# Expert outputs scaled at the PSUM evacuation and scattered with addition into two accumulators

## What is computed

```
xn = layernorm(x)
s  = attention branch of RWKV form: k, v, r projections of token-shifted xn,
     a running exponential average over the 512 tokens (the scan), then (r * rwkv) @ Wo.T
probs = softmax(xn @ w_router.T)              # 16 experts
top_w, top_e = top_k(probs, 4); top_w /= sum(abs(top_w))
moe = 0
for e in range(16):
    coeff = sum(where(top_e == e, top_w, 0))
    h = silu(xn @ w_gate[e]) * (xn @ w_up[e])
    moe = moe + coeff[:, None] * (h @ w_down[e])
out = x + s * silu(moe)
```

## Time and profile before

| | |
|---|---|
| median of 3 runs | 364.33 us (363.87 to 364.96) |
| profiled execution, first to last instruction | 374.3 us |
| PE, DVE, ACT, POOL busy | 83%, 76%, 39%, 61% of the span |
| granted TensorE clock, mean | 0.946 of full speed |
| moved by DMA | 48.81 MB, mean 130 GB/s |

### The profile page before, as it was taken

The page is one execution under the profiler, slowest core; times in us unless marked ns, Lnnn a source line. Parts: engine busy times, 40 slices in busy tenths (PEclk is TensorE's granted clock), DMA queues, the critical chain, the costliest instruction groups (busy, mean ns, idle before and its releaser), DMA issues.

```text
span 374.3 us, 4815 instructions
## 1 busy us (share of the span) xinstructions
PE 310.6 (83%) x1162; PEld 183.0 (49%) x1163; DVE 282.9 (76%) x534; ACT 146.0 (39%) x222; POOL 227.3 (61%) x231
## 2 busy tenths in 40 slices
...
GB/s 248 300 343 348 345 5 0 90 164 44 154 42 83 84 48 94 143 78 70 73 78 135 42 84 80 79 93 132 73 79 85 213 189 331 48 234 125 133 112 113
DMA packets 37894, 48.81 MB, mean 130 GB/s; under 512 B 3756, under 2 KB 33453, under 8 KB 37872
## 3 DMA queue, kind: packets, MB, share of 16 engines
...
...
## 4 chain that ended last, share of the span: by engine, by line
PE 43%; DVE 33%; issue 8%; DMA 4%; POOL 3%; ACT 3%; another core or an unknown queue 2%; SPq 1%; DVEq 1%; POOLq 0%; ACTq 0%
PE ps L588 36%; DVE wbig L1042 6%; DVE ohA L924 5%; PE ps L690 3%; PE ps L677 3%; DVE ohB L922 2%; POOL y_rows L411 2%; DMA xg<-xn_rows,tok_idx 2%; DMA woT<-woT_in 2%; DVE arena L954 1%; POOL xg L404 1%; PE ps L597 1%; DVE arena L815 1%; DVE arena L949 1%
## 5 line engine op out<-in xcount | busy, mean ns | idle before, releaser
L588 PE MATMUL ps<-wbig,arena 128*128 x576 | 206.3, 499 | 10.6 <-DVE arena L949 6.8
L588 PEld LDWEIGHTS ps<-wbig,arena 128*128 128x128 f32 x576 | 105.2, 195 | 74.5 <-issue 67.4
L411 POOL DMA_INDIRECT y_rows<-arena,s_idx x56 | 62.2, 1110 | 42.3 <-ACT arena L541 25.5
L404 POOL DMA_INDIRECT xg<-xn_rows,g_idx x64 | 70.3, 1099 | 22.8 <-issue 17.0
L954 DVE TENSOR_TENSOR arena<-arena,ps 128x512 f32<-128x512 f32 x36 | 24.5, 682 | 41.9 <-ACT arena L536 25.9
L536 ACT ACTIVATE arena<-ps 128x512 f32<-128x512 f32 x36 | 21.5, 597 | 87.0 <-PE ps L588 53.2
L588 PE MATMUL ps<-arena 128*128 128x512 f32 x96 | 47.1, 638 | 1.0 <-DVE arena L815 1.0
L949 DVE COPY arena<-ps 128x512 f32<-128x512 f32 x36 | 24.8, 690 | 26.3 <-PE ps L690 18.2
L541 ACT COPY arena<-ps 128x512 f32<-128x512 f32 x36 | 21.1, 585 | 45.8 <-PE ps L588 35.9
L690 PEld LDWEIGHTS ps<-ident,arena 128*128 128x128 f32 x144 | 18.4, 145 | 22.6 <-issue 19.3
L588 PEld LDWEIGHTS ps<-arena 128*128 128x128 f32 x96 | 18.6, 202 | 21.5 <-issue 19.4
(11 more groups left out here) (151 smaller groups left out, 385.6 us busy)
## 6 DMA issues: line engine op xcount, KB each, us to landing
...
```

The costliest lines, as they stand in the source:

```text
L404: pool.indirect_dma_start(out=xg[:, par, j, :], out_offset=None, in_=xn_rows, in_offset=bass.IndirectOffsetOnAxis(ap=idx[:, n + j:n + j + ...
L411: pool.indirect_dma_start(out=y_rows, in_=ysb[:, par, j, :], in_offset=None, out_offset=bass.IndirectOffsetOnAxis(ap=idx[:, n + j:n + j + ...
L588: ins = nc.tensor.matmul(dst, lhsT(c), rhs(c), start=(c == 0), stop=(c == C - 1))
```

## The change

Every expert output is scaled by its token's coefficient when ACT takes it out of PSUM, and it is scattered with addition (`compute_op=ALU.add`) into one of two DRAM accumulators of 2048 rows, `moe[0]` for the first tile of a pair and `moe[1]` for the second. 128 rows more take the padding.

- The coefficients of all 16 experts are computed before the second mix and stored behind each token's row in `xn_rows` (272 instead of 256 numbers), so a gather brings them along; ACT keeps them for four pairs in `kept` and picks the tile's expert by a register.
- SP fills both accumulators with zeros early.
- A scatter waits until the scatter of the pair before into the same accumulator has landed, since two of them may hold the same token.
- One table of places is enough; sign and slot work goes away, and so do slot loads, the counts for them, and the sums over slots.
- After the last scatter SP loads both accumulators in 8 chunks; per chunk DVE adds them, multiplies by s after ACT's silu, and adds the residual. POOL has no part in the tail.

The diff, cut to its core:

```diff
-    xn_rows = nc.dram_tensor("xn_rows", [TOK, D], f32, kind="Internal").ap()
-    y_rows = nc.dram_tensor("y_rows", [ROWS, D], f32, kind="Internal").ap()
+    xn_rows = nc.dram_tensor("xn_rows", [TOK, D + E], f32, kind="Internal").ap()
+    moe = [nc.dram_tensor(f"moe{j}", [TOK + P, D], f32, kind="Internal").ap() for j in range(2)]
...
+        kept = sb("kept", [P, 4 * 2 * E])
...
-        y4 = wbig[:, 0:T * TOPK * D].rearrange("p (s t n) -> p t s n", t=T, s=TOPK)
-        acc = wbig[:, T * TOPK * D:T * (TOPK + 1) * D].rearrange("p (t n) -> p t n", t=T)
-        assert (TOPK - 1) * T * D <= (E - TOPK + 1) * 2 * C * D and T * TOPK * D <= 2 * C * E * D
+        wsel, coef = eq, gt
+        accs = [wbig[:, j * T * D:(j + 1) * T * D].rearrange("p (t n) -> p t n", t=T) for j in range(2)]
...
-        table = [ps[:, B_HT, 0:NT], ps[:, B_XT, 0:NT]]
+        table = ps[:, B_HT, 0:NT]
...
             sp.dma_start(wdn[:, 0, 0:early_e], wd_v[0][:, 0:early_e]).then_inc(wdn_in, 16)
+            sp.wait_ge(weights_ready, 1)
+            sp.dma_start(coef_v, coef).then_inc(coef_stored, 16)
+            sp.wait_ge(zeros_ready, 1)
+            for j in range(2):
+                sp.dma_start(moe_v[j], zeros[:, :].unsqueeze(1).to_broadcast([P, T + 1, D])).then_inc(moe_zeroed, 16)
             sp.wait_ge(experts_ready, 1)
+            sp.wait_ge(coef_stored, 16)
             sp.dma_start(wdn[:, 0, early_e:], wd_v[0][:, early_e:]).then_inc(wdn_in, 16)
             sp.dma_start(wdn[:, 1, 0:E - LATE], wd_v[1][:, 0:E - LATE]).then_inc(wdn_in, 16)
             sp.wait_ge(index_ready, 1)
-            sp.wait_ge(slots_known, 3)
-            sp.wait_ge(weights_ready, 1)
+            sp.wait_ge(slots_known, 1)
             sp.dma_start(wdn[:, 1, E - LATE:], wd_v[1][:, E - LATE:]).then_inc(wdn_in, 16)
...
-            for s in range(TOPK - 1):
-                if s == TOPK - 2:
-                    reload(BATCH - 1)
-                for par in range(2):
-                    sp.wait_ge(y_out[par], counts[2 * s + par])
-                sp.dma_start(y4[:, :, s, :], y_v[:, :, s, :]).then_inc(y_in[s], 16)
             sp.wait_ge(y_psum, pairs)
-            for i in range(2):
-                sp.wait_ge(y_out[i], scattered)
+            for j in range(2):
+                sp.wait_ge(y_out[j], scattered)
             for n in range(T // 2):
-                sp.dma_start(y4[:, 2 * n:2 * n + 2, TOPK - 1, :], y_v[:, 2 * n:2 * n + 2, TOPK - 1, :]).then_inc(y_last_in[n], 16)
+                for j in range(2):
+                    sp.dma_start(accs[j][:, 2 * n:2 * n + 2, :], moe_v[j][:, 2 * n:2 * n + 2, :]).then_inc(moe_in[n], 16)
             for n in range(T // 2):
                 sp.wait_ge(res_ready, n + 1)
-                sp.dma_start(out_v[:, 2 * n:2 * n + 2, :], acc[:, 2 * n:2 * n + 2, :]).then_inc(out_stored, 16)
+                sp.dma_start(out_v[:, 2 * n:2 * n + 2, :], accs[0][:, 2 * n:2 * n + 2, :]).then_inc(out_stored, 16)
...
+            pool.memset(zeros[:, :], 0.0).then_inc(zeros_ready, 1)
...
             def gather(i, par, idx, n):
                 wait_alone(xt_psum, i - 1)
+                wait_alone(coef_kept, i - 1)
                 for j in range(2):
                     pool.indirect_dma_start(out=xg[:, par, j, :], out_offset=None, in_=xn_rows,
                                             in_offset=bass.IndirectOffsetOnAxis(ap=idx[:, n + j:n + j + 1], axis=0)
@@ -408,19 +397,16 @@
             def scatter(i, par, idx, n):
                 wait_alone(y_ready, i + 1)
                 for j in range(2):
-                    pool.indirect_dma_start(out=y_rows, in_=ysb[:, par, j, :], in_offset=None,
+                    wait_alone(y_out[j], 16 * i)
+                    pool.indirect_dma_start(out=moe[j], in_=ysb[:, par, j, :], in_offset=None,
                                             out_offset=bass.IndirectOffsetOnAxis(ap=idx[:, n + j:n + j + 1], axis=0),
-                                            bounds_check=last_row, oob_is_err=False).then_inc(y_out[par], 16)
-            last_row = pool.to_reg(ROWS - 1)
+                                            compute_op=ALU.add).then_inc(y_out[j], 16)
...
-            def add(n, a, b, ready):
-                pool.tensor_tensor(acc[:, 2 * n:2 * n + 2, :], a, b, ALU.add).then_inc(ready, 1)
-            for n in BACK:
-                tt = slice(2 * n, 2 * n + 2)
-                pool.wait_ge(scaled_ready, n - BACK[0] + 1)
-                add(n, y4[:, tt, 0, :], y4[:, tt, 1, :], half_ready)
-            for n in BACK:
-                tt = slice(2 * n, 2 * n + 2)
-                pool.wait_ge(half_ready, n - BACK[0] + 1)
-                pool.wait_ge(scaled_ready, len(BACK) + n - BACK[0] + 1)
-                add(n, acc[:, tt, :], y4[:, tt, 2, :], back_ready)
-            pool.wait_ge(xre_in, 16 * (T // 2))
-            for n in range(T // 2):
-                pool.wait_ge(ffn_times_s, n + 1)
-                add(n, acc[:, 2 * n:2 * n + 2, :], xre[n], res_ready)
...
+                nc.scalar.copy(kept[:, 2 * E * ring:2 * E * (ring + 1)].rearrange("p (j e) -> p j e", j=2),
+                               xg[:, par, :, D:]).then_inc(coef_kept, 1)
...
-            def evac_y(i, par, before):
+            def evac_y(i, par, ring):
                 act.wait_ge(y_psum, i + 1)
-                wait(act, y_out[par], 16 * before)
-                nc.scalar.copy(ysb[:, par].rearrange("p j n -> p (j n)"), ps[:, B_Y, :]).then_inc(y_ready, 1)
+                act.wait_ge(coef_kept, i + 1)
+                for j in range(2):
+                    wait(act, y_out[j], 16 * (i - 1))
+                for j in range(2):
+                    e = act.value_load(tile_expert[0:1, bass.ds(2 * i + j, 1)], min_val=0, max_val=E - 1)
+                    ins = nc.scalar.activation(ysb[:, par, j, :], ps[:, B_Y, j * D:(j + 1) * D], ACT.Copy,
+                                               scale=kept[:, bass.ds((ring * 2 + j) * E + e, 1)])
+                ins.then_inc(y_ready, 1)
...
-            act.wait_ge(y_in[0], 16)
-            act.wait_ge(y_in[1], 16)
-            for slots in ((0, 1), (2,)):
-                if slots == (2,):
-                    act.wait_ge(y_in[2], 16)
-                for n in BACK:
-                    for t in (2 * n, 2 * n + 1):
-                        for k in slots:
-                            ins = nc.scalar.activation(y4[:, t, k, :], y4[:, t, k, :], ACT.Copy, scale=coef4[:, t, k:k + 1])
-                    ins.then_inc(scaled_ready, 1)
...
             link(V.tensor_tensor_scan(flat(slot), flat(keep), flat(sel), 0.0, ALU.mult, ALU.add))
-            link(V.tensor_tensor(slot, slot, sel, ALU.mult))
+            V.tensor_tensor(slot, slot, sel, ALU.mult)
+            link(V.tensor_tensor(wsel, prob, sel, ALU.mult))
+            link(V.tensor_reduce(wsum, wsel, X, ALU.add))
+            link(V.reciprocal(winv, wsum))
+            V.tensor_tensor(coef, wsel, inner(winv), ALU.mult).then_inc(weights_ready, 1)
             dve.wait_ge(decay_ready, 1)
             V.tensor_scalar(decay[:, :], decay[:, :], -1.0, None, ALU.mult)
             mixes(1)
...
-            V.tensor_scalar(high[:, :], table[1], 0.0, float(2 * TOK), ALU.not_equal, ALU.mult)
-            link(V.tensor_copy(signed[:, :], table[0]))
-            link(V.tensor_tensor(signed[:, :], signed[:, :], table[1], ALU.add))
-            V.tensor_scalar(padt, signed[:, :], 0.0, padv, ALU.is_equal, ALU.mult)
-            link(V.scalar_tensor_tensor(out=token[:, :], in0=signed[:, :], scalar=-1.0, in1=signed[:, :], op0=ALU.mult, op1=ALU.max))
-            link(V.scalar_tensor_tensor(out=dst_idx[:, :], in0=token[:, :], scalar=-1.0, in1=padt, op0=ALU.add, op1=ALU.add))
+            link(V.tensor_scalar(padt, table, 0.0, padv, ALU.is_equal, ALU.mult))
+            link(V.scalar_tensor_tensor(out=dst_idx[:, :], in0=table, scalar=-1.0, in1=padt, op0=ALU.add, op1=ALU.add))
...
-            V.tensor_copy(token[:, :], dst_idx[:, :])
-            link(V.tensor_scalar(odd[:, :], signed[:, :], 0.0, float(TOK), ALU.is_lt, ALU.mult))
-            link(V.tensor_tensor(token[:, :], token[:, :], odd[:, :], ALU.add))
-            V.tensor_tensor(dst_idx[:, :], token[:, :], high[:, :], ALU.add).then_inc(dst_ready, 1)
             slots_done()
...
-            row_weights()
...
-            def weighted(n, k):
-                for t in (2 * n, 2 * n + 1):
-                    if k == 0:
-                        ins = V.tensor_scalar(acc[:, t, :], y4[:, t, 0, :], coef4[:, t, 0:1], None, ALU.mult)
-                    else:
-                        ins = V.scalar_tensor_tensor(out=acc[:, t, :], in0=y4[:, t, k, :], scalar=coef4[:, t, k:k + 1],
-                                                     in1=acc[:, t, :], op0=ALU.mult, op1=ALU.add)
-                return ins
-            for k in range(TOPK - 1):
-                dve.wait_ge(y_in[k], 16)
-                for n in FRONT:
-                    ins = weighted(n, k)
-                link(ins)
```

(27 more changed lines are left out.)

87 lines of the change are left out of this document (35 added, 52 removed).

## The result

| | before | after |
|---|---|---|
| median, same chip | 364.64 us (363.87 to 366.26) | 388.33 us (387.35 to 389.85) |
| ratio | | 1.064, 95% interval 1.060 to 1.068 |

The change makes the kernel slower by 23.7 us. The forecast was 358; the time lies within the range of 353 to 390 that the rivals opened, and rival 1 has come true: POOL became the bound of the loop.

The account below looks back on a forecast made before the run. DVE was taken to bound routing and tail, PE the loop, with POOL's queue close behind. Terms 1.6 + 3 + 1 - 4 - 8 = -6.4 us on the 374.3 us span, carried over to the 364.33 median: 358 us, range 353 to 390.

Parts of the forecast that it names:

- rival 1: Expert loop: POOL becomes the bound if an adding scatter costs x more; x = 0.5 gives 374 us; chance 0.33.
- scatters with addition: POOL's queue in the loop: an adding scatter costs +0.2 us (bounds 0 to +1.0), 0 after POOL's slack.
- Routing: Before the second mix, where DVE is the bound: four instructions move there from covered work, +1.6 us.
- ACT in the loop: Register loads and split copies delay the exponential 0.8 us, 0.4 lost in each of seven pairs: +3 us (0 to 14).
- ACT's code: ACT's program grows from 183 to 464 listed rows; one or two more instruction fetches, +1 us (0 to 7).
- The slots' loads leave: Mid-loop near 300 us: no 2 MB slot load holds up a gather and PE any more, -4 us (0 to -4.2).
- The tail: After the last scatter: DVE's 24 additions of 0.60 us without POOL beside it, -8 us (-4 to -10).
- rival 2: Loop: the scatter's new wait for landing sets the pace from a landing of 5.0 us; 394 us at 6.3; chance 0.08.
- Rival 3: Loop: ACT paces the exponential pairs with register loads of 1.5 us, +11, 369 us; chance 0.07.
- Rival 4: Tail gives less: loads feed DVE slowly, landing takes 3 us longer, -3 instead of -8, 363 us; chance 0.07.

Follow-up runs that it names:

- e1_plain: The changed kernel with plain scatters instead of adding ones, so the sum over experts is left out; 364.65 us, ratio 1.001 to the kernel before.
- b1_before: The kernel before, unchanged, run again for a second profile (span 362.2 us); 365.38 us, ratio 1.001.

## Why the prediction was wrong

**The step that failed** is *scatters with addition*: "I take +0.2, that is 0 after POOL's slack". Measured: 1.00 us for a plain scatter in its shortest rows, 1.60 for an adding one, +0.60, inside the bounds of 0 to 1.0 but above the 0.32 at which it ate the gain. The argument for a small value was that gather and scatter cost the same though their indirect side differs, hence a mostly fixed cost. That compares two plain transfers with one list each; it says nothing of an addition. What of it takes POOL 0.60 us more was not tested. The trace shows only that a scatter's rows then go in 128 packets instead of 32, one for each row. I had named a rule with rival 1, of the Trainium skill ("Collectives: The Full Stack", Part 3, why ReduceScatter is half of AllGather): two read descriptors for an addition. The trace does not bear it out: it shows packets and no descriptors, and a scatter's large packets become four times as many, not twice; that the queue's total about doubles (7008 to 13920) comes from the 74 gathers, which stay as they were.

Rival 1's own formula gives at x = 0.60: 28 x (2 x 0.60 - 0.42) = 21.8 us. The addition cost 24.0 us, 2.6 of them in the tail and 18.3 in the 28 pairs from the first exponential to the last: the mechanism was worked out rightly, and given too small a chance. That the size fits so well is in part luck. The formula goes from 6.04 to 5.62 + 1.20 = 6.82 us per pair; measured were 178.66/28 = 6.38 without the addition and 196.93/28 = 7.03 with it, both slower.

**Routing, +1.6.** The four instructions took DVE 38.56 to 40.16 us, and the mixes behind them started at 40.16 instead of 38.85, 1.3 later. But the last of this did not reach the loop: the first transposes came at 91.95 instead of 91.87 (92.90 in e1_plain). 0 to 1 us.

**ACT in the loop, +3.** 6.0 us over seven blocks. The load before the first activation is 0.84 us at most (I took 0.7), the gap before the second 0.25. The size of a load was right; that DVE's and PE's queued work would cover 0.4 of 0.8 us was not: the whole delay came through.

**ACT's code, +1.** No wait for anything unnamed is in the changed kernel: 0. The waits which I read as fetches of instructions are the unexplained stalls; no run shows that they are fetches.

**The slots' loads leave, -4.** 0.6 us: from the last exponential to the last transposes 34.72 instead of 35.28. The 4 us were read off a single execution, and the second one shows less of them: its transposes there are at 284.29, 291.15, 298.39 and 304.43, 2.0 us above three paces of 6.04. A part of the first one's loss was not the wait itself but the clock behind it. In the first profile PE waited 1.00 us for the gather's rows and 0.88 more behind the transposes; after that the granted clock averaged 0.60 over 4 us, so it stood at its lower level (1.2 of 2.4 GHz) for most of them, and the next four matmuls took 3.05 us. In b1_before the first wait was 0.62 us, the clock stayed at 1.00, and they took 1.98. Window of the first profile, its row of matmuls, then both of b1_before:

```profile
302.50:306.50 4.00, 3.94 (x9) 2.15 (x10) 0.69 (x1) 0.00 (x0) 3.09 (x4) 0.60 0.29 95
302.56 3.05 PE L588 MATMUL ps<-wbig,arena 128*128 x4 [0.88 <-issue]
...
292.50:296.50 4.00, 3.81 (x12) 2.02 (x13) 1.48 (x3) 0.14 (x1) 3.13 (x3) 1.00 0.48 165
292.69 1.98 PE L588 MATMUL ps<-wbig,arena 128*128 x4 [0.88 <-ACT arena L531]
```

**The tail, -8.** -7.1 with plain scatters, -4.5 with adding ones. Loads were issued 2.19 us after the last scatter's end (359.40 to 361.59), where I had 1.8; each adding scatter took 0.6 longer; the 24 steps of DVE at 0.60 us stood as forecast. (In the forecast's sum of the loads 343.8 + 14.9 is 358.7 and not 359.7, so that path would have ended at 361.3; DVE's own, to 361.3 and a few waits, is not touched.)

**Sum.** In e1_plain 1.1 (later start) + 6.0 - 0.6 - 7.1 = -0.6 us; I had -6.4. So even without the failed step the change would have been no gain, since two more terms were wrong in size: the slots' loads, taken at -4 and measured at -0.6, and ACT in the loop, taken at +3 and measured at +6.0.

**Rivals 2 to 4.** No scatter on POOL waits for a landing: rival 2 did not occur, with 3.9 us from issue to landing and 7 us between scatters of one accumulator. Rival 3 came about by a quarter: ACT's term was 3 us above the forecast's, not 11. Rival 4: DVE waited for DMA at the first two chunks, and for 0.20 us at the third.
